# Fused graph transformer on one core: inputs of the leading shared groups loaded ahead, mid norms in two runs, the last graph's routing one group sooner

## What is computed

```python
x = x + gated_graph_conv(layernorm(x), adj)   # degree norm, adj @ (x theta), gate sigmoid, elu
x = x + moe_ffn(layernorm(x))                 # a shared FFN and 2 of 8 experts, 128 -> 512 -> 128, exact gelu
x = x + attention_gnn(layernorm(x), adj)      # 4 heads, sigmoid scores times adj, layernorm
x = x + sliced_hydra(layernorm(x))            # soft slices, a state space mixer, deslicing
```

```python
shared = gelu(x @ W1s + b1s) @ W2s + b2s
rw = softmax(x @ Wr); topw, topi = top_k(rw, 2); topw = topw / topw.sum()
priv = gelu(x @ W1p[e] + b1p[e]) @ W2p[e] + b2p[e]      # for the two chosen experts e
out = shared + sum over the two of topw * priv
```

## Time and profile before

| | |
|---|---|
| median of 3 runs | 1588.74 us |
| the profiled execution | 1589.47 us, of which its span (first to last instruction) 1587.8 us |
| granted TensorE clock, mean | 0.969 of full |
| busy share of the span | TensorE matmuls 89%, VectorE 63%, ScalarE 47%, GpSimd 46% |
| 257.5 to 333 us of the span | the leading shared groups beside the last graph's routing |
| 343.5 to 357.9 us | leading groups 8 and 9 |
| 357.9 us on | first row transposes, then 71 routed groups |

### The profile page before, as it was taken

One profiled execution on the slowest core, in us unless ns is written; L12 is line 12 of the kernel. 1 busy time (PEld: TensorE's weight loads), 2 busy tenths in 40 slices (PEclk: granted clock), 3 DMA queues, 4 the chain that ended last, 5 costly groups with the idle time before them and its releaser, 6 DMA issues. The chain is left out here.

```text
span 1587.8 us, 25057 instructions
## 1 busy us (share of the span) xinstructions
PE 1412.8 (89%) x9010; PEld 813.4 (51%) x9010; DVE 1005.5 (63%) x2206; ACT 748.7 (47%) x1186; POOL 736.1 (46%) x504
## 2 busy tenths in 40 slices
PE   4999997879999999967699988998997589999998
PEld 2455554649999998712122222222222267774488
DVE  2468767433333333349689899999996578876723
ACT  3466565423444444355364554655553167773110
POOL 1127766630000000578887887875224378881000
PEclk9999999989999999989899999999998799999999
DMA  9667733466777775534342423433321231004024
GB/s 297 239 229 262 237 98 126 148 189 176 233 226 233 233 225 173 148 98 125 91 131 87 125 83 122 139 93 105 107 75 52 59 109 28 14 1 87 1 82 133
DMA packets 207311, 215.13 MB, mean 135 GB/s; under 512 B 23237, under 2 KB 164421, under 8 KB 207188
## 3 DMA queue, kind: packets, MB, share of 16 engines
q1 hardware_dynamic: 198996, 196.67, 40.6%
q0 software_dynamic: 8192, 16.86, 3.3%
HBM read 168.41 MB, written 45.07 MB: 134 GB/s over the span
## 5 line engine op out<-in xcount | busy, mean ns | idle before, releaser
L1342 ACT ACTIVATE c_AH<-c_S 128x2048 f32<-128x2048 f32 x128 | 240.6, 1880 | 245.6 <-PE c_S L1233 245.6
L1372 DVE TENSOR_TENSOR c_AH<-c_AH,c_A 128x2048 f32<-128x2048 f32 x128 | 312.5, 2450 | 45.5 <-ACT c_AH L1342 45.1
L1167 POOL DMA_INDIRECT c_G<-ys,slots x112 | 207.9, 1857 | 32.9 <-issue 31.0
L753 ACT ACTIVATE a_A<-a_DG,a_A 128x256 f32<-128x256 f32 (+1 forms) x194 | 95.0, 529 | 218.5 <-PE a_DG L626 217.4
L1233 PE MATMUL c_S<-c_Q,c_K 32*128 32x512 f32 x1024 | 150.9, 660 | 20.6 <-ACT c_AH L1342 8.8
L1258 PE MATMUL c_DG<-c_AH,c_ones 128*32 128x512 f32 x1024 | 139.3, 617 | 26.1 <-DVE c_AH L1372 26.1
L490 POOL DMA_INDIRECT rows<-a_S,a_slots x128 | 133.9, 1046 | 58.8 <-issue 45.5
L517 POOL DMA_INDIRECT a_A<-ys,slots x16 | 16.4, 1023 | 306.0 <-DMA ys<-a_A 301.5
L626 PE MATMUL a_DG<-a_A 128*128 128x256 f32 (+1 forms) x388 | 126.8, 450 | 20.2 <-DMA a_A<-xT_all 11.5
L1246 PE MATMUL c_YA<-c_AH,c_XT 128*32 128x512 f32 x1024 | 137.0, 616 | 6.5 <-DVE c_XT L1420 6.5
L597 PE MATMUL a_AG<-a_A,x 128*128 128x512 f32 x256 | 114.1, 598 | 5.1 <-DVE a_Z L826 5.1
(11 more groups left out here) (338 smaller groups left out, 2484.8 us busy)
## 6 DMA issues: line engine op xcount, KB each, us to landing
a_A<-in_dram SPq DMA_DIRECT2D x72, 578.0 KB, 3.9
a_A<-in_dram SPq DMA_DIRECT2D x32, 1024.0 KB, 9.8
c_A<-in_dram SPq DMA_DIRECT2D x128, 256.0 KB, 2.8
a_A<-rows SPq DMA_DIRECT2D x71, 129.0 KB, 3.2
ys<-a_A SPq DMA_DIRECT2D x71, 128.0 KB, 2.2
a_X<-in_dram SPq DMA_DIRECT2D x8, 512.0 KB, 12.6
a_R<-in_dram SPq DMA_DIRECT2D x8, 512.0 KB, 4.9
stream<-a_R SPq DMA_DIRECT2D x8, 512.0 KB, 9.8
```

The costliest lines, as they stand in the source:

```text
L753: act.activation(hT[g % 2][:, f, 0:size(g)], up_bank(g, f)[:, 0:size(g)], ACT.Gelu, bias=w_of(g)[:, F_N + f:F_N + f + 1]).then_inc(h_ready, 1)
L1167: pool.indirect_dma_start(Gt[k][:, t, :], None, ys, bass.IndirectOffsetOnAxis(ap=slots[:, k, T * i + t:T * i + t + 1], axis=0), bounds_che ...
L1342: act.activation(AH[g % UNITS][:, :, :], S[:, :, :], ACT.Sigmoid, scale=HD ** -0.5).then_inc(att_ready, 1)
L1372: dve.tensor_tensor(ah[:, :, :], ah[:, :, :], A[g % ADJ_BUFS][:, :].unsqueeze(1).to_broadcast([P, HEADS, HALF]), ALU.mult).then_inc(ah_dve, 1)
```

## The change

- `left` names seven buffers of the first block (both X, xn, dpart, one H, one Z, and F, which is x0). They take the transposed input and the residual rows of leading groups 3 to 9, each with a semaphore of its own. `load_lead` loads them, on SyncE's queue, right behind those of groups 0 to 2, each once its buffer has had its last reader in the first block. The leading loads between stores are gone.
- Y has 6 buffers (NY) instead of 3, so that their stores can lag.
- SyncE stores the x2T of graph 5 behind four of these loads, `fill_ends` behind the store of group 1, `begin_routed` behind that of group 3, `begin_rows` behind that of group 7.
- `normalise_mid` takes the copy k. For graph 6 the first copy stands ahead of ScalarE's second aggregate copy, the second behind gelu(0). For graph 7 the first stands ahead of gelu(2), the second behind copy_x2T(7). For graphs 0 to 5 both runs follow each other as before.
- Graph 7's x2_transposes stand ahead of down(1) instead of behind it, its logits ahead of up(3), its rank behind up(3). Its x2T goes to the buffer aggT.
- VectorE does choose(7), place(7) and make_table ahead of read_y(2).

The diff, cut to its core (the rest passes NY and the new names on):

```diff
 ROWS = E_N * CAP + E_N * G
-NW, NR = 5, 9
+NW, NR, NY = 5, 9, 6
 i32, u32 = mybir.dt.int32, mybir.dt.uint32
...
         xT = [carve(0, u * GS, [GS]) for u in range(3)]
-        Y = [carve(0, (3 + u) * GS, [ST, D]) for u in range(3)]
-        Rr = [carve(0, (6 + u) * GS, [ST, D]) for u in range(3)]
-        past = carve(0, 9 * GS, [ROUTED, E_N])
-        passed = carve(0, 9 * GS + ROUTED * E_N, [ROUTED, E_N])
-        hit = carve(0, 9 * GS + 2 * ROUTED * E_N, [E_N, K_MAX])
+        Rr = [carve(0, (3 + u) * GS, [ST, D]) for u in range(3)]
+        Y = [carve(0, (6 + u) * GS, [ST, D]) for u in range(NY)]
+        past = carve(0, (6 + NY) * GS, [ROUTED, E_N])
+        passed = carve(0, (6 + NY) * GS + ROUTED * E_N, [ROUTED, E_N])
+        hit = carve(0, (6 + NY) * GS + 2 * ROUTED * E_N, [E_N, K_MAX])
+        left = {3: X[0], 4: X[1], 5: xn, 7: Hh[0], 8: Z[0], 9: F}
+        left = {g: a[:, :, :].rearrange("p t d -> p (t d)") for g, a in left.items()}
+        left[6] = dpart[:, :]
         Wb = [carve(1, u * BLOB, [BLOB]) for u in range(NW)]
...
         def shared_count(g):
-            return 16 * sum(1 for p in range(g % 3, g + 1, 3) if not is_routed(p))
+            return 16 * sum(1 for p in range(g % 3, g + 1, 3) if not is_routed(p) and p not in left)
+
+        def xT_of(g):
+            return left[g][:, 0:GS] if g in left else xT[g % 3]
+
+        def mid_of(g):
+            return left[g][:, GS:2 * GS].rearrange("p (t d) -> p t d", t=ST) if g in left else Rr[g % 3]
+
+        def shared_in(engine, sems, g):
+            if g in left:
+                engine.wait_ge(lead_loaded[g], 32)
+            else:
+                engine.wait_ge(sems[g % 3], shared_count(g))
+
+        def x2T_of(r):
+            return aggT if r == B - 1 else x2T[r % 2]
...
                 sp.wait_ge(x2T_ready, NH * i + NH)
-                sp.dma_start(xT_all[i], x2T[i % 2][:, :]).then_inc(xT_stored, 16)
+                sp.dma_start(xT_all[i], x2T_of(i)[:, :]).then_inc(xT_stored, 16)
...
                 load_r(i)
-                if i >= 2:
+                if 2 <= i < B - 1:
                     store_xT(i - 2)
+
+            def load_lead(g):
+                i, part = divmod(g, N // GS)
+                sp.wait_ge(xT_stored, 16 * (i + 1))
+                sp.dma_start(xT_of(g), xT_all[i, :, bass.ts(part, GS)]).then_inc(lead_loaded[g], 16)
+                sp.wait_ge(mid_stored, 16 * (i + 1))
+                sp.dma_start(mid_of(g), tiled(mid_rows[bass.ts(g, GS), :])).then_inc(lead_loaded[g], 16)
...
                 to = ys[bass.ts(g - LEADING, G), :] if is_routed(g) else sums[bass.ts(shared_of(g), GS), :]
-                sp.dma_start(tiled(to), Y[g % 3][:, 0:size(g) // P, :]).then_inc(y_stored[g % 3], 16)
+                sp.dma_start(tiled(to), Y[g % NY][:, 0:size(g) // P, :]).then_inc(y_stored[g % NY], 16)
...
                 load_shared(g)
+            sp.wait_ge(xn_ready, B)
+            load_lead(3)
+            load_lead(4)
+            sp.wait_ge(degT_psum, B)
+            load_lead(6)
+            sp.wait_ge(xnT_psum, NH * B)
+            load_lead(5)
+            store_xT(B - 3)
             store_mid(B - 2)
+            load_lead(7)
+            load_lead(8)
+            sp.wait_ge(agg_psum, NH * B)
+            load_lead(9)
             store_xT(B - 2)
-            for g in range(3, 6):
-                load_shared(g)
-                store_y(g - 3)
             store_mid(B - 1)
+            store_y(0)
             store_xT(B - 1)
-            for g in range(6, LEADING):
-                if g == LEADING - 2:
-                    fill_ends()
-                load_shared(g)
-                store_y(g - 3)
+            store_y(1)
+            fill_ends()
+            store_y(2)
+            store_y(3)
             begin_routed()
-            store_y(LEADING - 3)
+            for g in range(4, LEADING - 2):
+                store_y(g)
             begin_rows()
...
                 for t in range(T):
-                    mm = pe.matmul(LG[:, t, :], x2T[r % 2][:, t * P:(t + 1) * P], Wg[:, :], start=True, stop=True)
+                    mm = pe.matmul(LG[:, t, :], x2T_of(r)[:, t * P:(t + 1) * P], Wg[:, :], start=True, stop=True)
                 mm.then_inc(logits_psum, 1)
...
             up(2)
+            x2_transposes(B - 1)
             down(1)
-            x2_transposes(B - 1)
+            logits(B - 1)
             up(3)
+            rank(B - 1)
             down(2)
-            logits(B - 1)
-            up(4)
-            down(3)
-            rank(B - 1)
-            for g in range(5, GROUPS):
+            for g in range(4, GROUPS):
                 up(g)
...
             def copy_x2T(r):
-                if r >= 2:
+                if 2 <= r < B - 1:
                     act.wait_ge(xT_stored, 16 * (r - 1))
...
                     act.wait_ge(x2T_psum, NH * r + h + 1)
-                    act.activation(x2T[r % 2][:, half(h)], FG[:, h, :], ACT.Copy).then_inc(x2T_ready, 1)
+                    act.activation(x2T_of(r)[:, half(h)], FG[:, h, :], ACT.Copy).then_inc(x2T_ready, 1)
...
-            def normalise_mid(i):
+            def normalise_mid(i, k):
                 act.wait_ge(shift2, i + 1)
...
                     act.wait_ge(sent[i % 3], 256 * (i // 3))
-                for k in range(2):
-                    for t in range(T):
-                        ins = act.activation(S[i % 3][k][:, t, 0:D], R[i % 2][:, t, :], ACT.Identity,
-                                             bias=shift[1][:, t:t + 1], scale=n2.rstd[i % 2][:, t:t + 1])
-                    ins.then_inc(s_ready, 1)
+                for t in range(T):
+                    ins = act.activation(S[i % 3][k][:, t, 0:D], R[i % 2][:, t, :], ACT.Identity,
+                                         bias=shift[1][:, t:t + 1], scale=n2.rstd[i % 2][:, t:t + 1])
+                ins.then_inc(s_ready, 1)
...
                     copy_dpart(i + 1)
+                if i >= 1:
+                    normalise_mid(i - 1, 0)
+                if 1 <= i < B - 1:
+                    normalise_mid(i - 1, 1)
                 if i == B - 1:
                     copy_agg(i, 1)
-                if i >= 1:
-                    normalise_mid(i - 1)
                 if i >= 2:
...
             gelu(0)
+            normalise_mid(B - 2, 1)
             elu_exp(B - 1)
...
             share(B - 2)
-            normalise_mid(B - 1)
+            normalise_mid(B - 1, 0)
             gelu(2)
             copy_x2T(B - 1)
+            normalise_mid(B - 1, 1)
             gelu(3)
-            gelu(4)
             share(B - 1)
-            for g in range(5, GROUPS):
+            for g in range(4, GROUPS):
                 gelu(g)
...
             def read_y(g):
-                u, tiles = g % 3, size(g) // P
+                u, tiles = g % NY, size(g) // P
                 dve.wait_ge(dn_psum, g + 1)
-                if g >= 3:
-                    dve.wait_ge(y_stored[u], 16 * (g // 3))
+                if g >= NY:
+                    dve.wait_ge(y_stored[u], 16 * (g // NY))
                 y, found = Y[u][:, 0:tiles, :], YB[g % 2][:, 0:tiles, :]
...
             read_y(1)
-            read_y(2)
             choose(B - 1)
-            read_y(3)
             place(B - 1)
             make_table()
+            read_y(2)
+            read_y(3)
             make_results()
```

More of the change, by code:

```diff
@@ L267, in front_stage @@
         mid_loaded = [sem(f"mid_loaded{u}") for u in range(3)]
+        lead_loaded = {g: sem(f"lead_loaded{g}") for g in range(3, LEADING)}
         xT_psum, xT_ready = sem("xT_psum"), sem("xT_ready")
@@ L270, in front_stage @@
         y_read, y_ready = sem("y_read"), sem("y_ready")
-        y_stored = [sem(f"y_stored{u}") for u in range(3)]
+        y_stored = [sem(f"y_stored{u}") for u in range(NY)]
         results_ready, pair_ready = sem("results_ready"), sem("pair_ready")
@@ L447, in _ @@
                     if g == LEADING + ROUTED:
-                        sp.wait_ge(y_stored[0], 16)
-                        sp.wait_ge(y_stored[1], 16)
+                        for g0 in range(N // GS):
+                            sp.wait_ge(y_stored[g0], 16)
                         sp.dma_start(x0[:, :, :], tiled(sums[0:N, :])).then_inc(x0_loaded, 16)
@@ L457, in _ @@
             sp.wait_ge(next_loaded, 48)
-            for u in range(3):
-                sp.wait_ge(y_stored[u], 16 * len(range(u, GROUPS, 3)))
+            for u in range(NY):
+                sp.wait_ge(y_stored[u], 16 * len(range(u, GROUPS, NY)))
         @block.gpsimd
@@ L512, in _ @@
             pool.wait_ge(results_ready, 1)
-            for u in range(3):
-                pool.wait_ge(y_stored[u], 16 * len(range(u, last + 1, 3)))
+            for u in range(NY):
+                pool.wait_ge(y_stored[u], 16 * len(range(u, last + 1, NY)))
             for m in range(2 * T):
@@ L614, in up @@
                 else:
-                    pe.wait_ge(xs_loaded[g % 3], shared_count(g))
+                    shared_in(pe, xs_loaded, g)
```

(6 more changed lines are left out.)

## The result

The changed kernel takes 1573.82 us (median of 4, 1572.29 to 1582.51) beside 1590.70 for the kernel before in its 4 runs (1586.99 to 1600.73): a ratio of 0.9894, 95% interval 0.9865 to 0.9923. The forecast was 1571.0 with 1567 to 1579. It counted 17.6 us down from 1588.74, the median of the first 3 runs before; with the fourth run (1592.66) that median is 1590.70, so 2.0 of the 2.8 us by which the forecast was low come from there, and the gain in medians is 16.9. The profiled execution took 1572.53 us against 1589.47, 16.9 less.

What follows compares the result with a forecast made beforehand. TensorE was taken to bound the kernel wherever it doesn't wait, so removed waits count in full: 5.2 us upstream plus 12.4 from loads and fills, 17.6 off 1588.74, forecast as 1571.0 us, range 1567 to 1579.

Steps and rivals of the forecast that it cites:

- Graph 6's norm in two runs: Before graph 6's transposes: x2_transposes(6) 2.5 us sooner, gelu(0) 3.6 sooner, but graph 7's exponential only 0.6 sooner.
- A new wait: In up(1), TensorE's gap before the second half grows from 1.64 to 5.0 us, with 1.5 us charged for slow clock.
- it costs nothing: The 1.5 us of slow clock after up(1)'s gap stays off the path, since up(2)'s second half must wait anyway.
- Graph 7's norm: At up(2): second half freed at 283.0 instead of 286.68, full clock behind it, bringing the upstream gain to 5.2 us.
- Routing a group sooner: Graph 7's transposes, logits and rank on TensorE: same instructions reordered without a wait, at worst costing up to 0.4 us.
- Leading inputs, fills: Around up(8): the 10.3 us load wait and 1.9 us of clock go, 12.4 us gained with 0.2 for rounding.
- Rows and scatters: Before the row transposes: wait stays 1.3 us, last scatter lands before rows are asked for, covered by 4.1 us.
- Six Y: Result buffers in the rows: six of them change nothing, since VectorE never waits for a store there.
- the upstream gain: Rival for the part before up(5): low clock or a moved wait loses the 5.2 us, giving 1576.3; chance 0.17.
- rival 2: GpSimd's scatters, blocked by VectorE's table work, land 6.7 us late and bound the rows: 1577.8; chance 0.10.
- The slower case: Rival at the scatters: all 40 issues slow to 2.10 us each, transposes 7.4 later, total 1596 or more; chance 0.03.
- the no-gain case: Rival at up(8): it waits as long for something else, so only the 5.2 us are gained, 1583.5; chance 0.05.

Runs made afterwards that it cites:

- the other set: Unaltered changed kernel run again beside three variants of it: 1616.33 us, ratio 0.9910 to the kernel before; kernels also run elsewhere took 33 to 43 us more there.

## Why the prediction was right, and where it was off

- **Graph 6's norm in two runs**: x2_transposes(6) at 258.43 (said 258.35), gelu(0) at 262.60 (262.6), exponential 0.54 sooner (0.6). Right.
- **A new wait**: at 273.55 after 4.72 us (said 273.5 after 5.0). The words "2.5 us earlier" and "0.6 earlier" would make it 3.5; up(1) started 3.6 sooner (266.87 for 270.48), and the 5.0 came from the 268.5. Its place was right and its cost was off, and this is where most of the 1.4 us went. I charged 1.5 us of low clock and let up(2)'s wait absorb them. Measured: 3.78 - 1.98 = 1.8 in up(1) and 4.84 - 3.73 = 1.1 in down(0), 2.9 together. So up(2) started only at 282.19 and ran without a stop, and its second half came at about 284.05, not 283.0. ScalarE was done with the half norm at 282.43 and then idle for 0.96 us until up(2)'s first result: TensorE, not ScalarE, set that time. The step that was off is "it costs nothing", with "283.0 at the latest": I had looked at four records behind a gap and not at what followed them. The 2.9 is one draw: the same gap cost 2.6 to 2.8 us in four more traces, and 1.6 in the changed kernel's trace of the other set (3.57, then 3.73). There up(2)'s second half waited 1.43 us for a Gelu ahead of which ScalarE had stood idle for 1.18, and came no sooner (49.0 from the mark, 48.8 here), so how much the full clock alone would give back isn't shown.
- **Graph 7's norm**: gained upstream 311.17 - 307.19 = **4.0 us, said 5.2**. The mechanism held, the term was too big by the clock.
- **Routing a group sooner**: on TensorE as said, without a wait (rank at 295.89, right behind up(3)). But pricing it at nothing asked only whether it adds a wait, not what hangs on it: the experiment without it lost 7.0 us. The forecast stood because it walked all edits together; its parts do not add up alone: loads 10.1, norms -0.2, loads and norms 9.1, loads and routing 9.6 (12.2 without the 2.6 of low clock), all three 16.2.
- **Leading inputs, fills**: from up(5) to the row transposes 46.71 us before and 34.52 now, **12.2, said 12.4**; the 0.2 is the rows' wait, 1.56 for 1.30. The load issues were not all "well under 1 us": three of the fourteen took 1.11 to 1.38 us, and no matmul waited for one.
- **Rows and scatters**: right, with more slack than I gave (some 7 us for 4.1). **Six Y**: nothing, as said.
- **Sum**: 16.2 at the transposes against 17.6; the span is 17.0 shorter, 0.8 more than at the transposes. It lies behind the second block, and I leave it open; that it makes up for part of the 1.4 is luck.
- **Rivals**: the upstream gain was not lost (4.0 of 5.2), though the clock it named took its share. The scatters did not bind; 9.2 us later they did, by 2.05. Beside VectorE's table (299 to 304 us) they kept their 0.30 us of idle time. So the stall of rival 2 did not come, which it would by the lock rule of the Trainium skill, SBUF — State Buffer, section "SBUF: two separate sides", if VectorE's operations had run in a two-port mode; the trace doesn't tell their mode, so the rule isn't tested. The slower case and the no-gain case did not come.
- **Chances**: the ratio is at 1.06% faster, its interval on both sides of 1%. I had put 0.57 above that line and 0.41 within.

## What to carry to other kernels

When a queue holds work that is bound to be late, moving one item past it can hand most of the wait to the next, as it did here (3.1 us gained of 12.2); look at every item behind it that has a deadline. Price edits in company: a reordering that adds no wait of its own can be what lets another edit pay, so walk the list again with each edit taken out. And when an edit makes an idle gap on TensorE, follow the clock through the work behind it until the durations are back, before saying that a later wait absorbs it.

## What the hardware showed that I had not expected

The same gap costs or does not cost. In front of graph 6's transposes TensorE waits 3.37 us in the kernel before and in the one with whole norms. Granted clock of that stretch in the first and in the second:

```profile
257.00:263.00 6.00, 2.63 (x22) 2.31 (x21) 2.28 (x10) 5.90 (x16) 1.81 (x2) 1.00 0.10 33
```

```profile
257.00:263.00 6.00, 2.63 (x15) 2.50 (x14) 2.28 (x10) 5.90 (x16) 1.81 (x2) 0.70 0.45 124
```

1.00 and 0.70; the transposes took 1.09 and 1.97 us. After gaps of 1.88 to 1.90 us four records took 1.98 in one run and 3.23 in another of the same kernel. The Trainium skill, TensorE: Matmul & The Clock Gate, section "What's actually happening", warns that the count of slow matmuls differs between runs of one kernel; the traces agree. In these traces the slow records behind a gap of 1.9 to 4.7 us took between 0 and 3.0 us more than at the full clock, and a single trace shows one draw.
